# Second graph layer in half blocks of 128 edges: 416 steps of the edge loop instead of 428, two additions per step, lag of two

## The chip, the cores and the metric

The kernel runs on one core of one Trainium2 chip. The metric is the device time of one execution in microseconds; lower is better. Engines are named as in the profile: PE (TensorE), DVE (VectorE), ACT (ScalarE), POOL (GpSimd), SP (SyncE, which only issues DMAs here).

## What is computed

A small network over 3125 nodes and 103125 directed edges sorted by target node: a three-layer mean-aggregation graph network, a mixture of 16 experts, a relational graph layer, and a mixture of 8 experts, each behind a layer norm and added to the stream. The change concerns the third of the four. Cut to what matters:

```
m     = clifford_linear(h[src] * r[edge_type], msg_w, msg_b)   # per edge
m     = m * sigmoid(r[edge_type] @ gate_w + gate_b) * norm(src, dst)
h_agg = segment_sum(m, dst)                                     # per node
h_out = clifford_linear(h + h_agg, upd_w, upd_b)
x     = x + h_out
```

The linear map commutes with the sum over edges, so the kernel first sums `h[src] * r[type]` (with the gate and the norm of the source multiplied into the rows) over the edges of each node, 257 numbers per edge (256 features and the factor itself for the bias), and applies the weights once per node afterwards.

## The kernel before

Nodes stand in 25 tiles of 128 (`NT`). The sorted edges, padded to 808 x 128, are cut into `BLOCKS` = 404 blocks of `BLOCK` = 256 edges. A block belongs to the tile of its first edge; edges of it that lie in a later tile fall outside its one-hot matrix. For each of the `EDGES_AT` = 24 borders between tiles an extra block is run a second time for the later tile: `total` = 404 + 24 = 428 steps.

`edge_blocks` (L361 to L472), early in the program beside other work, turns the sorted list into tables: `b_src` (row to gather, per partition), `b_near` (place of the target in its tile), `b_tile` (tile of a block), `b_start` (first edge of an extra block). They are saved to HBM and loaded before the first use in `build`.

`aggregate` (L547 to L663) is the edge loop. One step n does:

- SP (L594): one DMA brings 256 rows of `relation_rows` (1040 bytes each, written by earlier stages) to `rel`; partition p gets rows 2p and 2p+1, 2080 bytes in a row.
- POOL (L608): two indirect DMAs gather 128 rows of `h_table` each into `rows`, with indices from `b_src`. POOL may be `SLOTS` = 12 steps ahead of PE (L605).
- ACT (L575, L578): two activations give |place - column|, one gives the two one-hot matrices, up to six steps ahead.
- DVE (L629): `rows` times `rel`, in place, both in SBUF. Ahead of it DVE's sequencer reads the tile number of step n-3 from `b_tile` into a register (L637, `value_load`).
- PE (L657): two fp32 matmuls, summed in one PSUM bank of six; the profile shows each as two MATMUL records.
- DVE (L623): adds the bank of step n-3 (`LAG` = 3) to the accumulator of its tile, in SBUF.

The waits are on counters: `s_sum` counts steps that PE has finished (plus 13 to begin with), `s_acc` additions, `s_ready` products. `Beside` puts a little other work (weights, and the part of the update that needs no sum, one node tile every 14 steps) into the same loop on PE, ACT and DVE. All loops are unrolled in the program; each engine runs its own list in order.

Of the kernel before, what the change touches and what calls it, by code (L numbers as in the profile page):

```python
# [57 lines left out]
SLOTS, BANKS, LAG = 12, 6, 3  # L58
assert PARTS * PER_PART == BLOCKS
# [301 lines left out]
def edge_blocks(nc, c, loads, relation):  # L361
# [5 lines left out]
    block_bits = BLOCK.bit_length() - 1  # L367
    with Core(nc) as k:
        both = k.sb("eb_lists", [PARTS, 2, PER_PART, BLOCK])
        first_i = k.sb("eb_first_i", [PARTS, 2, PER_PART], I32)  # L370
        base = k.sb("eb_base", [PARTS, PER_PART])
# [4 lines left out]
        pick = k.sb("eb_pick", [PARTS, PER_PART, EDGES_AT])  # L376
        n4 = k.sb("eb_n4", [PARTS, 1])
        near = k.sb("eb_near_in", [PARTS, 1, PER_PART, BLOCK])
        shift = k.sb("eb_shift", [P, EDGES_AT])
        src_out = k.sb("eb_src", [P, BLOCKS + EDGES_AT, 2], I32)  # L380
        near_out = k.sb("eb_near", [P, BLOCKS + EDGES_AT, 2])
# [6 lines left out]
        with nc.Block() as block:  # L388
# [11 lines left out]
            def _(sp):  # L400
                sp.dma_start(start[:, :], c.tab["a_start_d"]).then_inc(s_start, 16)
                sp.dma_start(both[:, :, :, :], c.lists.rearrange("a (n b e) -> n a b e", n=PARTS, b=PER_PART)).then_inc(s_lists, 16)
# [7 lines left out]
                sp.dma_start(c.tab["b_src_d"], src_out[:, :, :].rearrange("p g k -> p (g k)")).then_inc(s_saved, 16)  # L410
                sp.dma_start(c.tab["b_near_d"], near_out[:, :, :].rearrange("p g k -> p (g k)")).then_inc(s_saved, 16)
# [4 lines left out]
            def _(dve):  # L416
# [4 lines left out]
                v.tensor_scalar(at[:, 0, :], starts, block_bits, block_bits, ALU.arith_shift_right, ALU.logical_shift_left)  # L421
                v.tensor_scalar(at[:, 1, :], starts, block_bits, None, ALU.arith_shift_right)
                st.link(v.tensor_scalar(at[:, 2, :], starts, BLOCK - 1, None, ALU.bitwise_and))
# [10 lines left out]
                v.tensor_tensor(near[:, 0, :, :], bc(base[:, :].unsqueeze(2), [PARTS, PER_PART, BLOCK]), both[:, 1, :, :], ALU.subtract).then_inc(s_near, 1)  # L434
                dve.wait_ge(s_spread, 1)
                st.link(v.tensor_scalar_mul(n4[:, :], spread[0:PARTS, 64:65], float(PER_PART)))
                st.link(v.tensor_scalar(own[:, :], spread[0:PARTS, 0:EDGES_AT], n4[:, 0:1], None, ALU.subtract))
                for b in range(PER_PART):
                    last = v.tensor_scalar(pick[:, b, :], own[:, :], float(b), None, ALU.is_equal)
# [4 lines left out]
                for q in range(4):  # L444
                    out = src_out if q < 2 else near_out
                    view = out[:, 0:BLOCKS, q % 2].rearrange("p (n b) -> p b n", b=PER_PART)
                    v.tensor_copy(view, turned[:, q, 0:BLOCKS].rearrange("p (b n) -> p b n", b=PER_PART))
                dve.wait_ge(s_turn, 2)
                for q in range(2):
                    v.tensor_copy(src_out[:, BLOCKS:, q], extra[:, q * 32:q * 32 + EDGES_AT])  # L450
                    last = v.tensor_tensor(near_out[:, BLOCKS:, q], shift[:, :], extra[:, 64 + q * 32:64 + q * 32 + EDGES_AT], ALU.subtract)
                last.then_inc(s_out, 1)

            @block.tensor
            def _(pe):
# [6 lines left out]
                for q in range(4):  # L462
                    for b in range(PER_PART):
                        src = both[:, 0, b, q % 2:BLOCK:2] if q < 2 else near[:, 0, b, q % 2:BLOCK:2]
# [3 lines left out]
                for q in range(4):  # L468
                    for b in range(PER_PART):
                        last = nc.tensor.matmul(extra[:, q * 32:q * 32 + EDGES_AT], both[:, q // 2, b, q % 2:BLOCK:2], pick[:, b, :],  # L470
                                                start=b == 0, stop=b == PER_PART - 1)
# [75 lines left out]
def aggregate(nc, c, name, table, width, acc, relation_rows, kernels, beside):  # L547
# [4 lines left out]
    total = BLOCKS + EDGES_AT  # L552
    with Core(nc) as k:
        rows = k.sb(f"{name}_rows", [P, SLOTS, 2, width])
        rel = k.sb(f"{name}_rel", [P, SLOTS, 2, width])
        gap = k.sb(f"{name}_gap", [P, BANKS, 2, P])
        onehot = k.sb(f"{name}_onehot", [P, BANKS, 2, P])
# [5 lines left out]
        with nc.Block() as block:  # L563

            @block.scalar
            def _(act):
# [3 lines left out]
                def places(n):  # L570
                    g = n

                    act.wait_ge(s_sum, g + (SLOTS + 2 - BANKS))
                    for t in range(2):
                        last = nc.scalar.activation(gap[:, n % BANKS, t, :], c.iota[:, 0:P], ACT.Abs, bias=c.tab["b_near"][:, bass.ds(g * 2 + t, 1)])  # L575
                    last.then_inc(s_gap, 1)
                    act.wait_ge(s_gap, g + 1)
                    nc.scalar.activation(onehot[:, n % BANKS, :, :], gap[:, n % BANKS, :, :], ACT.Relu, bias=1.0, scale=-1.0).then_inc(s_oh, 1)  # L578
# [10 lines left out]
            def _(sp):  # L589
                def relation(n, start):  # L590

                    sp.wait_ge(s_sum, (n + 2))
                    src = relation_rows[bass.ds(start, BLOCK), :].rearrange("(p k) c -> p (k c)", p=P)
                    sp.dma_start(rel[:, n % SLOTS, :, :].rearrange("p k c -> p (k c)"), src).then_inc(s_rel[n % SLOTS], 16)  # L594
# [20 lines left out]
            def _(dve):  # L615
                v = nc.vector

                def add(g, bank, tile):

                    dve.wait_ge(s_acc, g + BANKS)  # L620
                    dve.wait_ge(s_sum, g + (SLOTS + 2 - LAG))
                    here = acc[:, bass.ds(tile, 1), 0:used].rearrange("p a d -> p (a d)")
                    v.tensor_tensor(here, here, sums[:, bank, 0:used], ALU.add).then_inc(s_acc, 1)  # L623

                def block_of(g, n, uses, tile):
                    dve.wait_ge(s_rel[n % SLOTS], uses * 16)
                    dve.wait_ge(s_rows[n % SLOTS], uses * 32)
                    here = rows[:, n % SLOTS, :, 0:used]
                    v.tensor_tensor(here, here, rel[:, n % SLOTS, :, 0:used], ALU.mult).then_inc(s_ready, 1)  # L629
                    add(g, (n - LAG) % BANKS, tile)  # L630

                v.memset(c.tab["b_tile"][:, 0:LAG], NT).then_inc(s_acc, 1)
                v.memset(acc[:, :, :], 0.0).then_inc(s_acc, BANKS - 1)
                dve.wait_ge(s_acc, BANKS)
                for n in range(total):
                    if n - LAG < BLOCKS:
                        tile = dve.value_load(c.tab["b_tile"][0:1, n:n + 1], min_val=0, max_val=NT)  # L637
                    else:
                        tile = n - LAG - BLOCKS + 1
                    block_of(n, n, n // SLOTS + 1, tile)  # L640
                    beside.vector(dve, v, n)
                for n in range(total, total + LAG):
                    add(n, (n - LAG) % BANKS, n - LAG - BLOCKS + 1)

            @block.tensor
            def _(pe):

                for q in range(LAG):
# [1657 lines left out]
def build(nc, I, out):  # L2306
    with Core(nc) as c:
# [19 lines left out]
        block_tables = {"b_src": ([P, (BLOCKS + EDGES_AT) * 2], I32), "b_near": ([P, (BLOCKS + EDGES_AT) * 2], F32),  # L2327
# [110 lines left out]
```

## Time and profile before

| | us |
|---|---|
| median of 3 runs | 3507.81 (3500.52 to 3517.4) |
| the profiled execution | 3519.02, of it span 3517.0 |
| edge loop of the second graph layer, first gather to last addition | 1798.6 to 2929.4 |
| POOL busy over the span | 2005.0 (57%) |
| PE busy over the span | 2505.9 (71%) |
| DVE, ACT busy over the span | 1375.3 (39%), 1405.1 (40%) |

The edge loop is about a third of the span. Shares over the whole span say little about it; the rows further down are taken from inside it. Columns of a group of instructions: line, engine, operation, output<-input, count, then busy time in total and mean of one, then the idle time of the engine just before such instructions and what ended most of it.

### The profile page before, as it was taken

To read this page: it belongs to the slowest core of one execution; us is meant where nothing else is said; L and a number is where in the kernel's file an instruction comes from. 1 tells how busy PE (TensorE), PEld (TensorE's weight loads), DVE (VectorE), ACT (ScalarE), POOL (GpSimd) and SP (SyncE) were. 2 spreads that over 40 slices of the span, in tenths; PEclk is the share of its full clock that TensorE was granted. 3 is DMA by queue.
4 is the path that set the end of the run, shared out by engine and by line. 5 is a ranking of instruction groups with operands and counts; after the bars stand their busy time and mean duration, and the time that the engine had idled before them with its cause. 6 is when DMAs were issued, how large, how long until landed. Compare 5 with 4: busy or idle time off the path is not lost. (4 is left out here: it accounts for less than half of the span.)

```text
span 3517.0 us, 51132 instructions
## 1 busy us (share of the span) xinstructions
PE 2505.9 (71%) x14080; PEld 1923.5 (55%) x14080; DVE 1375.3 (39%) x4123; ACT 1405.1 (40%) x3615; POOL 2005.0 (57%) x1969
## 2 busy tenths in 40 slices
PE   0156899999999847886016666666667667499997
PEld 0123566678888746875014444444444445488986
DVE  4167789942221150000864444444444445500100
ACT  0035666646740022322034444444444443255554
POOL 0454767667777136653647777777777771033332
PEclk9998999999999958998557766776766667599998
DMA  2674676678888336665347777777777771354233
GB/s 111 202 253 122 199 211 197 209 220 263 265 259 243 105 118 190 186 200 156 96 152 211 202 206 198 200 206 204 200 203 203 203 207 59 117 174 129 37 82 62
DMA packets 343366, 620.94 MB, mean 177 GB/s; under 512 B 82286, under 2 KB 157565, under 8 KB 342241
## 3 DMA queue, kind: packets, MB, share of 16 engines
q1 hardware_dynamic: 236033, 343.11, 30.2%
q0 software_dynamic: 101360, 268.76, 28.9%
q10 hardware_dynamic: 5728, 6.11, 0.5%
q8 instruction: 115, 1.88, 0.2%
q14 instruction: 130, 1.06, 0.1%
HBM read 451.74 MB, written 170.90 MB: 177 GB/s over the span
## 5 line engine op out<-in xcount | busy, mean ns | idle before, releaser
L608 POOL DMA_INDIRECT agg_r_rows<-h_table,parts_and_x x856 | 864.9, 1010 | 315.3 <-issue 217.6
L657 PE MATMUL agg_r_sums<-agg_r_rows,agg_r_onehot 128*128 128x257 f32 x1712 | 702.3, 560 | 388.9 <-DVE agg_r_rows L629 329.1
L657 PEld LDWEIGHTS agg_r_sums<-agg_r_rows,agg_r_onehot 128*128 128x128 f32 x1712 | 432.3, 276 | 645.6 <-issue 580.4
L1414 POOL DMA_INDIRECT rl_buf<-r_table,kinds x608 | 626.6, 1031 | 261.9 <-issue 171.4
L629 DVE TENSOR_TENSOR agg_r_rows<-agg_r_rows,agg_r_rel 128x514 f32<-128x514 f32 x428 | 298.9, 698 | 649.8 <-DMA agg_r_rows<-h_table,parts_and_x 648.0
L575 ACT ACTIVATE agg_r_gap<-iota,parts_and_x 128x128 f32<-128x128 f32 x856 | 295.2, 392 | 520.8 <-PE agg_r_sums L657 489.8
L1784 PE MATMUL f_pH<-f_xT,f_w 128*128 128x128 f32 x2816 | 369.4, 292 | 79.5 <-DMA f_w<-in_L_ffn_w 55.5
L1784 PEld LDWEIGHTS f_pH<-f_xT,f_w 128*128 128x128 f32 x2816 | 353.6, 205 | 110.9 <-DMA f_w<-in_L_ffn_w 60.3
L1136 PE MATMUL ly_acc<-parts,matrix 128*128 128x256 bf16 x1250 | 342.2, 274 | 0.0
L1135 PE MATMUL ly_acc<-parts,matrix 128*128 128x256 bf16 x1250 | 340.4, 272 | 0.0
L1134 PE MATMUL ly_acc<-parts,matrix 128*128 128x257 bf16 (+1 forms) x1250 | 340.2, 272 | 0.0
L1869 ACT ACTIVATE f_hT<-f_pH,f_b 128x128 f32<-128x128 f32 x704 | 197.8, 372 | 345.6 <-PE f_pH L1784 345.3
L1803 PE MATMUL f_pY<-f_w,f_hT 128*128 128x256 f32 x1408 | 327.1, 382 | 0.0
L1803 PEld LDWEIGHTS f_pY<-f_w,f_hT 128*128 128x128 f32 x1408 | 262.1, 193 | 30.9
L2022 POOL DMA_INDIRECT f_xb<-xn_table,f_token x120 | 118.2, 985 | 246.0 <-DVE f_home L1970 116.3
L2010 POOL DMA_INDIRECT f_ys<-f_yb,f_home x56 | 88.2, 1575 | 294.6 <-DVE f_yb L1995 263.7
L1272 DVE TENSOR_SCALAR b_oh<-b_numbers,b_code 128x400 bf16<-128x400 f16 x980 | 254.6, 324 | 0.0
L1123 PE MATMUL b_strips<-b_oh,b_at 128*128 128x400 bf16 x980 | 200.8, 336 | 63.4 <-DVE b_oh L1272 30.3
L1414 POOL DMA_INDIRECT f_rr_buf<-r_table,kinds x120 | 121.4, 1012 | 150.7 <-POOLq L113 112.8
L623 DVE TENSOR_TENSOR acc<-acc,agg_r_sums 128x257 f32 (+1 forms) x431 | 179.2, 416 | 13.2 <-PE agg_r_sums L657 13.1
L578 ACT ACTIVATE agg_r_onehot<-agg_r_gap 128x256 f32<-128x256 f32 x428 | 178.3, 416 | 13.5
L1989 DVE TENSOR_TENSOR f_plain<-f_pY,f_b 128x256 f32<-128x256 f32 x56 | 23.8, 424 | 380.5 <-PE f_pY L1803 380.5
(389 smaller groups left out, 3543.2 us busy)
## 6 DMA issues: line engine op xcount, KB each, us to landing
agg_r_rel<-relation_rows SPq DMA_DIRECT2D x428, 260.0 KB, 3.1
relation_rows<-rl_buf SPq DMA_DIRECT2D x304, 260.0 KB
f_w<-in_L_ffn_W SPq DMA_DIRECT2D x28, 1024.0 KB, 5.8
f_w<-in_L_ffn_w SPq DMA_DIRECT2D x38, 512.0 KB, 5.9
relation_rows<-f_rr_buf POOLq DMA_DIRECT2D x60, 260.0 KB, 2.6
agg_r_rows<-h_table,parts_and_x POOLq DMA_INDIRECT x856, 3.4
ly_zin<-zh SPq DMA_DIRECT2D x50, 256.0 KB
zh<-ly_out SPq DMA_DIRECT2D x50, 256.0 KB, 2.7
```

The costliest lines, as they stand in the source:

```text
L575: last = nc.scalar.activation(gap[:, n % BANKS, t, :], c.iota[:, 0:P], ACT.Abs, bias=c.tab["b_near"][:, bass.ds(g * 2 + t, 1)])
L608: pool.indirect_dma_start(rows[:, n % SLOTS, t, :], None, table, bass.IndirectOffsetOnAxis(ap=indices[:, t:t + 1], axis=0)).then_inc(s_row ...
L629: v.tensor_tensor(here, here, rel[:, n % SLOTS, :, 0:used], ALU.mult).then_inc(s_ready, 1)
L657: last = nc.tensor.matmul(sums[:, n % BANKS, 0:used], onehot[:, n % BANKS, t, :], rows[:, n % SLOTS, t, 0:used], start=t == 0, stop=t == 1)
L1123: last = nc.tensor.matmul(strips[:, n % BANKS, 0:CODES], at[:, n % 2, t, :], oh[:, n % 2, t, :], start=t == 0, stop=t == DEEP - 1)
L1134: nc.tensor.matmul(acc[:, n % 2, 0:D + one], m[:, s, own], of[:, s, 2 * D:3 * D + one], start=s == 0, stop=False)
L1135: nc.tensor.matmul(acc[:, n % 2, 0:D], m[:, s, own], of[:, s, 0:D], start=False, stop=False)
L1136: last = nc.tensor.matmul(acc[:, n % 2, 0:D], m[:, s, own], of[:, s, D:2 * D], start=False, stop=s == NT - 1)
L1272: last = v.tensor_scalar(oh[:, n % 2, t, :], numbers[:, :], code[:, q, 1, own, t:t + 1], None, ALU.is_equal)
L1414: pool.indirect_dma_start(self.buf[:, n, g, :], None, self.table, bass.IndirectOffsetOnAxis(ap=self.c.kinds[:, at:at + 1], axis=0)).then_i ...
L1784: last = nc.tensor.matmul(pH[s][:, f * P:(f + 1) * P], w1b[:, s, h, f * P:(f + 1) * P], xT[:, s, h, :], start=h == 0, stop=h == KD - 1)
L1803: last = nc.tensor.matmul(pY[s][:, 0:D], hT[:, s, f, :], w2b[:, s, f, :], start=f == 0, stop=f == FC - 1)
```

## The change

Halves of 128 edges take the place of the block as the unit that belongs to a tile: `HALVES` = 808. A step still handles 256 edges, now two halves, each with a tile of its own, so each half has a PSUM bank and an addition of its own. The 24 borders need 24 extra halves, which make 12 steps; `total` = 404 + 12 = 416. `LAG` goes from 3 to 2, so six banks hold three steps of two banks. `HOT` = 6 keeps the ring of one-hot matrices as it was. The relation rows of a half go one to a partition: 1040 bytes to `rel[p, 0]` and 1040 to `rel[p, 1]`, from places 128 rows apart; an extra step fetches its two halves with two DMAs from two start addresses. DVE reads two tile numbers per step, and it does so behind the product of the step. `edge_blocks` builds the tables in the new order.

```diff
-SLOTS, BANKS, LAG = 12, 6, 3
+SLOTS, BANKS, LAG, HOT = 12, 6, 2, 6
+HALVES, PER_HALF = 2 * BLOCKS, 2 * PER_PART
...
-    total = BLOCKS + EDGES_AT
+    total = BLOCKS + EDGES_AT // 2
...
                 for n in range(BLOCKS):
-                    relation(n, n * BLOCK)
+                    sp.wait_ge(s_sum, n + 2)
+                    src = relation_rows[n * BLOCK:(n + 1) * BLOCK, :].rearrange("(k p) c -> p k c", p=P)
+                    sp.dma_start(rel[:, n % SLOTS, :, :], src).then_inc(s_rel[n % SLOTS], 16)
                 for n in range(BLOCKS, total):
-                    relation(n, sp.value_load(c.tab["b_start"][0:1, n - BLOCKS:n - BLOCKS + 1], min_val=0, max_val=EDGE_TILES * P))
+                    starts = [sp.value_load(c.tab["b_start"][0:1, at:at + 1], min_val=0, max_val=EDGE_TILES * P)
+                              for at in (2 * (n - BLOCKS), 2 * (n - BLOCKS) + 1)]
+                    sp.wait_ge(s_sum, n + 2)
+                    for t in range(2):
+                        sp.dma_start(rel[:, n % SLOTS, t, :], relation_rows[bass.ds(starts[t], P), :]).then_inc(s_rel[n % SLOTS], 16)
...
+                def tile_of(half):
+                    at = half + 2 * LAG
+                    return dve.value_load(c.tab["b_tile"][0:1, at:at + 1], min_val=0, max_val=NT) if half < HALVES else half - HALVES + 1
+                def add(n):
+                    tiles = [tile_of(2 * (n - LAG) + t) for t in range(2)]
+                    dve.wait_ge(s_sum, n + (SLOTS + 2 - LAG))
+                    for t in range(2):
+                        dve.wait_ge(s_acc, 2 * n + t + BANKS)
+                        here = acc[:, bass.ds(tiles[t], 1), 0:used].rearrange("p a d -> p (a d)")
+                        v.tensor_tensor(here, here, sums[:, (2 * (n - LAG) + t) % BANKS, 0:used], ALU.add).then_inc(s_acc, 1)
...
-                for q in range(LAG):
+                for q in range(2 * LAG):
                     last = nc.tensor.matmul(sums[:, BANKS - 1 - q, 0:used], c.zero_b[:, 0:P], c.zero_b[:, 0:used], start=True, stop=True)
...
-                    pe.wait_ge(s_acc, g + (LAG + 1))
+                    pe.wait_ge(s_acc, 2 * (g + LAG + 1))
...
-                        last = nc.tensor.matmul(sums[:, n % BANKS, 0:used], onehot[:, n % BANKS, t, :], rows[:, n % SLOTS, t, 0:used],
-                                                start=t == 0, stop=t == 1)
+                        last = nc.tensor.matmul(sums[:, (2 * n + t) % BANKS, 0:used], onehot[:, n % HOT, t, :], rows[:, n % SLOTS, t, 0:used],
+                                                start=True, stop=True)
```

On DVE, in the middle of the edge loop, one step before the change reads as follows: the register load of a tile number, the product, the register operations that carry the waits of the addition, the addition. `acc1` is the accumulator, `b_tile` the table of tile numbers.

```order
L637 TENSOR_LOAD b_tile
L637 ISA x2
L629 TENSOR_TENSOR agg_r_rows<-agg_r_rows,agg_r_rel 128x2x257
L623 ISA
L623 TENSOR_TENSOR acc1<-acc1,agg_r_sums 128x257
```

The same engine and place with the change (L642 is the product, L623 the tile number, L633 the addition):

```order
L642 TENSOR_TENSOR agg_r_rows<-agg_r_rows,agg_r_rel 128x2x257
L623 TENSOR_LOAD b_tile
L623 ISA x2
L623 TENSOR_LOAD b_tile
L623 ISA x2
L633 ISA
L633 TENSOR_TENSOR acc1<-acc1,agg_r_sums 128x257
L633 ISA
L633 TENSOR_TENSOR acc1<-acc1,agg_r_sums 128x257
```

Two loads with their register operations now stand between the product and the first addition; before, the one load stood between an addition and the next product.

On SP, the relation rows: first the 404 regular steps, then one extra step, before the change.

```order
L594 DMA agg_r_rel<-relation_rows 128x520 x404
L599 TENSOR_LOAD parts_and_x
L599 ISA x2
L594 ISA
L594 DMA agg_r_rel<-relation_rows 128x520
```

With the change:

```order
L592 DMA agg_r_rel<-relation_rows 128x2x260 x404
L594 TENSOR_LOAD parts_and_x
L594 ISA x2
L594 TENSOR_LOAD parts_and_x
L594 ISA x2
L598 ISA
L598 DMA agg_r_rel<-relation_rows 128x260
L598 ISA
L598 DMA agg_r_rel<-relation_rows 128x260
```

Each regular DMA carries the same bytes in twice as many pieces; an extra step loads two start addresses and issues two DMAs of half the size.

## Rows read from the trace of the kernel before

**Rows 1.** Page, part 5: groups of the edge loop on POOL, PE, DVE, ACT.
```profile
L608 POOL DMA_INDIRECT agg_r_rows<-h_table,parts_and_x x856 | 864.9, 1010 | 315.3 <-issue 217.6
L657 PE MATMUL agg_r_sums<-agg_r_rows,agg_r_onehot 128*128 128x257 f32 x1712 | 702.3, 560 | 388.9 <-DVE agg_r_rows L629 329.1
L629 DVE TENSOR_TENSOR agg_r_rows<-agg_r_rows,agg_r_rel 128x514 f32<-128x514 f32 x428 | 298.9, 698 | 649.8 <-DMA agg_r_rows<-h_table,parts_and_x 648.0
L575 ACT ACTIVATE agg_r_gap<-iota,parts_and_x 128x128 f32<-128x128 f32 x856 | 295.2, 392 | 520.8 <-PE agg_r_sums L657 489.8
L623 DVE TENSOR_TENSOR acc<-acc,agg_r_sums 128x257 f32 (+1 forms) x431 | 179.2, 416 | 13.2 <-PE agg_r_sums L657 13.1
L578 ACT ACTIVATE agg_r_onehot<-agg_r_gap 128x256 f32<-128x256 f32 x428 | 178.3, 416 | 13.5
```

**Rows 2.** Line 608, its gathers: duration in ns min/median/max, first and last start.
```profile
L608 POOL DMA_INDIRECT agg_r_rows<-h_table,parts_and_x x856: 949/953/1472, 1798.6 to 2923.1; - x172
```

**Rows 3.** Timeline of the loop's end: start, duration, engine, [idle before <-what ended it].
```profile
2916.56 0.42 DVE L623 TENSOR_TENSOR acc<-acc,agg_r_sums 128x257 f32<-128x257 f32 x1
...
2916.83 0.95 POOL L608 DMA_INDIRECT agg_r_rows<-h_table,parts_and_x  x1 [0.31 <-issue]
...
2926.57 1.33 DVE L623 TENSOR_TENSOR acc<-acc,agg_r_sums 128x257 f32<-128x257 f32 x3
...
2926.81 2.05 PE L657 MATMUL agg_r_sums<-agg_r_rows,agg_r_onehot 128*128 128x257 f32 x4 [0.43 <-DVE agg_r_rows L629]
2928.97 0.42 DVE L623 TENSOR_TENSOR acc<-acc,agg_r_sums 128x257 f32<-128x257 f32 x1 [1.06 <-PE agg_r_sums L657]
```

**Rows 4.** Timelines of POOL and DVE where a gather is long and where not.
```profile
2033.44 1.29 POOL L608 DMA_INDIRECT agg_r_rows<-h_table,parts_and_x  x1 [0.30 <-issue]
...
2033.22 0.69 DVE L629 TENSOR_TENSOR agg_r_rows<-agg_r_rows,agg_r_rel 128x514 f32<-128x514 f32 x1 [1.83 <-DMA agg_r_rows<-h_table,parts_and_x]
...
2603.13 0.95 POOL L608 DMA_INDIRECT agg_r_rows<-h_table,parts_and_x  x1 [0.30 <-PE agg_r_sums L657]
2603.25 0.69 DVE L629 TENSOR_TENSOR agg_r_rows<-agg_r_rows,agg_r_rel 128x514 f32<-128x514 f32 x1 [1.37 <-DMA agg_r_rows<-h_table,parts_and_x]
```

**Rows 5.** Line 637, the register load on DVE's sequencer: ns min/median/max.
```profile
L637 DVEq TENSOR_LOAD <-b_tile x407: 298/304/330, 1804.0 to 2869.5; - x136
L637 DVEq FUSED_REGOPS  x407: 190/190/190, 1804.4 to 2869.9; - x136
L637 DVEq SEQ_ASSERT  x407: 23/23/33, 1804.6 to 2870.1; - x136
```

**Rows 6.** Timeline of DVE: two steps back to back, and additions in a chain.
```profile
2515.35 0.70 DVE L629 TENSOR_TENSOR agg_r_rows<-agg_r_rows,agg_r_rel 128x514 f32<-128x514 f32 x1 [2.98 <-DMA agg_r_rows<-h_table,parts_and_x]
2515.96 0.42 DVE L623 TENSOR_TENSOR acc<-acc,agg_r_sums 128x257 f32 x1
2516.30 0.69 DVE L629 TENSOR_TENSOR agg_r_rows<-agg_r_rows,agg_r_rel 128x514 f32<-128x514 f32 x1
...
2509.61 0.41 DVE L2287 TENSOR_TENSOR parts_and_x<-parts_and_x,be_result 128x256 f32<-128x256 f32 x1
2510.06 0.42 DVE L2289 TENSOR_TENSOR parts_and_x<-parts_and_x,upd_bias 128x256 f32<-128x256 f32 x1
```

**Rows 7.** DMA queues and issues from 2000 to 2800 us: packets, MB, share of 16 engines.
```profile
q0 software_dynamic: 29118, 80.81, 38.0%
q1 hardware_dynamic: 43742, 80.89, 34.0%
...
agg_r_rel<-relation_rows SPq DMA_DIRECT2D x304, 260.0 KB, 3.0
agg_r_rows<-h_table,parts_and_x POOLq DMA_INDIRECT x609, 3.4
```

**Rows 8.** DMA queue from 1790 to 1797 us, a store of 1040-byte rows.
```profile
q1 hardware_dynamic: 656, 0.67, 27.3%
```

**Rows 9.** Timeline: that store's issue, and the matmuls ahead of the first gather.
```profile
1792.18 0.36 SPq L2129 DMA_DIRECT2D h_table<-f_out  x1
...
1796.92 0.81 PE L649 MATMUL agg_r_sums<-zero_b 128*128 128x257 bf16 x3 [133.55 <-PEq L113]
```

**Rows 10.** Timeline of the end of `edge_blocks`.
```profile
165.71 0.17 DVE L451 TENSOR_TENSOR eb_near<-eb_shift,eb_extra 128x24 f32<-128x24 f32 x1
...
169.84 7.90 SPq L410 DMA_DIRECT2D b_src_d<-eb_src  x1
```

More of the change, by code:

```diff
@@ L57 @@
 PARTS, PER_PART = 101, 4
-SLOTS, BANKS, LAG = 12, 6, 3
-assert PARTS * PER_PART == BLOCKS
+SLOTS, BANKS, LAG, HOT = 12, 6, 2, 6
+HALVES, PER_HALF = 2 * BLOCKS, 2 * PER_PART
+assert PARTS * PER_PART == BLOCKS and EDGES_AT % 2 == 0 and BANKS % 2 == 0 and LAG < BANKS // 2
 E0, F0, TILES0 = 16, 512, (2 * N + 16 * (P - 1)) // P
@@ L433, in _ @@
                 st.link(v.tensor_scalar_mul(base[:, :], base[:, :], float(P)))
-                v.tensor_tensor(near[:, 0, :, :], bc(base[:, :].unsqueeze(2), [PARTS, PER_PART, BLOCK]), both[:, 1, :, :], ALU.subtract).then_inc(s_near, 1)
+                v.tensor_tensor(near[:, :, :], bc(base[:, :].unsqueeze(2), [PARTS, PER_HALF, P]), both[:, 1, :, :], ALU.subtract).then_inc(s_near, 1)
                 dve.wait_ge(s_spread, 1)
-                st.link(v.tensor_scalar_mul(n4[:, :], spread[0:PARTS, 64:65], float(PER_PART)))
+                st.link(v.tensor_scalar_mul(n4[:, :], spread[0:PARTS, 64:65], float(PER_HALF)))
                 st.link(v.tensor_scalar(own[:, :], spread[0:PARTS, 0:EDGES_AT], n4[:, 0:1], None, ALU.subtract))
-                for b in range(PER_PART):
+                for b in range(PER_HALF):
                     last = v.tensor_scalar(pick[:, b, :], own[:, :], float(b), None, ALU.is_equal)
@@ L445, in _ @@
                     out = src_out if q < 2 else near_out
-                    view = out[:, 0:BLOCKS, q % 2].rearrange("p (n b) -> p b n", b=PER_PART)
+                    view = out[:, 0:HALVES].rearrange("p (n b) -> p b n", b=PER_HALF)[:, (q % 2) * PER_PART:(q % 2 + 1) * PER_PART, :]
                     v.tensor_copy(view, turned[:, q, 0:BLOCKS].rearrange("p (b n) -> p b n", b=PER_PART))
                 dve.wait_ge(s_turn, 2)
[L449 to L452, printed above, removed]
+                v.tensor_copy(src_out[:, HALVES:], extra[:, 0:EDGES_AT])
+                v.tensor_tensor(near_out[:, HALVES:], shift[:, :], extra[:, 32:32 + EDGES_AT], ALU.subtract).then_inc(s_out, 1)
             @block.tensor
@@ L463, in _ @@
                     for b in range(PER_PART):
-                        src = both[:, 0, b, q % 2:BLOCK:2] if q < 2 else near[:, 0, b, q % 2:BLOCK:2]
+                        half = (q % 2) * PER_PART + b
+                        src = both[:, 0, half, :] if q < 2 else near[:, half, :]
                         last = nc.tensor.transpose(turned[:, q, b * PARTS:(b + 1) * PARTS], src, c.ident[0:PARTS, 0:PARTS])
@@ L467, in _ @@
                 pe.wait_ge(s_pick, 1)
[L468 to L471, printed above, removed]
+                for q in range(2):
+                    for b in range(PER_HALF):
+                        last = nc.tensor.matmul(extra[:, q * 32:q * 32 + EDGES_AT], both[:, q, b, :], pick[:, b, :],
+                                                start=b == 0, stop=b == PER_HALF - 1)
                 last.then_inc(s_turn, 1)
@@ L616, in _, with loads_of @@
                 v = nc.vector
[L618 to L632, printed above, removed]
+                def loads_of(n):
+                    slot = [q for q in range(n + 1) if q % SLOTS == n % SLOTS]
+                    return sum(16 if q < BLOCKS else 32 for q in slot)
+                def tile_of(half):
[8 more added lines that the diff above has]
+                        v.tensor_tensor(here, here, sums[:, (2 * (n - LAG) + t) % BANKS, 0:used], ALU.add).then_inc(s_acc, 1)
+                v.memset(c.tab["b_tile"][:, 0:2 * LAG], NT).then_inc(s_acc, 1)
                 v.memset(acc[:, :, :], 0.0).then_inc(s_acc, BANKS - 1)
@@ L635, in _ @@
                 for n in range(total):
[L636 to L640, printed above, removed]
+                    dve.wait_ge(s_rel[n % SLOTS], loads_of(n))
+                    dve.wait_ge(s_rows[n % SLOTS], (n // SLOTS + 1) * 32)
+                    here = rows[:, n % SLOTS, :, 0:used]
+                    v.tensor_tensor(here, here, rel[:, n % SLOTS, :, 0:used], ALU.mult).then_inc(s_ready, 1)
+                    add(n)
                     beside.vector(dve, v, n)
                 for n in range(total, total + LAG):
-                    add(n, (n - LAG) % BANKS, n - LAG - BLOCKS + 1)
+                    add(n)
             @block.tensor
             def _(pe):
-                for q in range(LAG):
+                for q in range(2 * LAG):
                     last = nc.tensor.matmul(sums[:, BANKS - 1 - q, 0:used], c.zero_b[:, 0:P], c.zero_b[:, 0:used], start=True, stop=True)
```

49 lines of the change are left out of this document (22 added, 27 removed).

## The prediction

> **What bounds the kernel now.** The change touches one stage, the edge loop, so I read that stage first by its groups [rows 1]. Per step of 256 edges (428 of them) the engines are busy: POOL 864.9 / 428 = 2.02 us, PE 702.3 / 428 = 1.64 us, DVE (298.9 + 179.2) / 428 = 1.12 us, ACT (295.2 + 178.3) / 428 = 1.11 us. None fills a step of about 2.6 us by busy time alone, so the idle columns decide. DVE's idle time ahead of the product is ended by the gathered rows landing (648.0 of 649.8 us), PE's mostly by DVE's product, ACT's by PE: all three wait down one chain that begins at POOL. POOL's own idle time is ended by "issue", and in the timelines each gap before a gather is 0.30 or 0.31 us, also where the page names PE as the releaser [rows 3, 4]: PE's count had been reached, and the 0.30 us is what POOL's own queue needs between two gathers. So POOL issues without a real wait from 1798.6 to 2923.1 us [rows 2], and its pace is the stage's: (2923.1 - 1798.6) / 855 = 1.315 us a gather, 2.63 us a step.
>
> A gather takes 0.95 us at the median but 1.010 in the mean, up to 1.47 [rows 1, 2]. The long ones sit where DVE's product had begun shortly before the gather (product at 2033.22, gather at 2033.44: 1.29 us); a product that begins after the gather does nothing to it (gather 2603.13, product 2603.25: 0.95 us) [rows 4]. An addition still running when a gather starts does not lengthen it either (2916.56 + 0.42 reaches past 2916.83; 0.95 us) [rows 3]. All this costs 856 x (1.010 - 0.953) = 49 us in the loop.
>
> **The change, part by part.**
>
> 1. *Twelve steps fewer.* 24 gathers go from the queue that sets the pace: 24 x 1.315 = 31.6 us less. The share of held gathers is inside the 1.315, and goes with the products, which also become 12 fewer. Everything else of those steps lay beside POOL.
>
> 2. *A second addition per step on DVE.* One reads PSUM and SBUF like the first, which did not hold a gather [rows 3]. The Trainium skill says the same and says why (SBUF — State Buffer, "Who interferes with whom"): a DVE instruction with at most one SBUF input doesn't contend with GpSimd, one with two SBUF inputs does contend with a GpSimd instruction that reads SBUF. It adds that a tensor_tensor had not been seen to stall a GpSimd-issued DMA; rows 4 show that it does here, and the measurement decides. By either the second addition costs POOL nothing.
>
> 3. *DVE's minimal step.* Today two products can follow each other by 0.95 us [rows 6], far below 2.63. Now the two tile numbers are read behind the product. One read is 0.304 + 0.190 + 0.023 us on DVE's sequencer, with gaps some 0.62 (the assert starts 0.6 us after the load: 1804.0 to 1804.6) [rows 5]. Does it run while the product does? 2515.35 to 2516.30 holds a product, an addition and a whole read, which fits into 0.95 us only if the read lies beside the product and the addition [rows 6]. So from the product's start: two reads to 1.3, register operations of the address and dispatch some 0.15 (estimate from the rest of the 0.95 us) to 1.5, the first addition; the second waits for it, as L2289 waits for L2287, 0.45 later [rows 6], 0.1 more for its own address: 2.05; the next product 0.34 us after an addition's start (2515.96 to 2516.30) [rows 6]: 2.4 us. Bounds: 1.53 = 0.70 + 2 x 0.416 if the reads cost nothing, 3.0 if they start only when the product has ended (0.70 + 1.24 + 0.13 + 0.55 + 0.34). I take 2.4, since rows 6 show the overlap. The update of a node tile adds 2 x 0.42 us every 14 steps, 0.05 a step: 2.45 against POOL's 2.63. DVE becomes 93% full but not the pace. Products will start later after landing now and then; POOL is allowed 12 steps ahead of PE and is now only some three ahead (landing 3.4 us, product 0.70, matmuls 2.05), so nine steps, over 20 us, hide that.
>
> 4. *Lag of two.* The additions of step n need the matmuls of n-2. Two minimal steps are 4.8 us; product and matmuls are 0.70 + 2.05 us [rows 3]: done 2 us before. PE waits for two more additions than before, but they stand on DVE ahead of the product that PE waits for anyway. Cost nil; the cover, should DVE get slower, grows with it. PE's work per step is the same two matmuls, only into two banks. Where its duration changed with the bank it would have 2.63 - 2.05 us of room.
>
> 5. *Relation rows in pieces of 1040 bytes.* 304 loads took 34.0% of 16 engines for 800 us: 0.34 x 16 x 800 / 304 = 14.3 us of engine time, 0.90 us of all 16 per step; per 2080-byte piece (128 a load) 112 ns under this load. The gathers: 38.0%, 1.00 us a step. Sum 1.90 of 2.63 us [rows 7]. Alone, a 1040-byte packet took 0.273 x 16 x 7 / 656 = 47 ns [rows 8]. Bounds for the new load: 256 x 47 / 16 = 0.75 us and 256 x 112 / 16 = 1.79 us (each small piece as long as a large one). The nearest row is the gathers, the same 1040-byte rows at the same bytes per step in the same stage: 1.00 us. I take that: DMA 2.0 of 2.63 us, not the bound. The load is issued nine steps ahead, so a longer landing costs nothing. SP needs 0.36 us to issue a DMA of 640 such rows [rows 9]; it has room.
>
> 6. *Extra steps on SP.* Two register loads and two DMAs per step, 12 times: under 2 us of SP in 2.63, and steps ahead. Nil.
>
> 7. *The ends.* One zero matmul more ahead of the first gather: 0.81 / 3 = 0.3 us [rows 9]. The last step ends with two additions: +0.5 us (part 3) on 2928.97 [rows 3].
>
> 8. *`edge_blocks`.* Four small comparisons more, a copy and an addition fewer; the tables are ready at 165.9 us, and SP stores them only from 169.8 [rows 10]: 4 us of cover. Nil; without it, well under 1 us.
>
> **Sum.** -31.6 + 0.3 + 0.5 = -30.8 us. The profiled execution of 3519.02 would take 3488.2. It lay 11.2 us above the median of the runs; from the median 3507.81 I get 3477.0 us, -0.88%. What a measurement can tell from no change is 0.5%, 17.5 us: faster is below 3490.3, slower above 3525.3.
>
> **Rivals.**
>
> A. *DVE becomes the pace, slower than before.* If the reads of tile numbers do not run beside the product, the step is 3.0 us plus 0.05: 416 x 3.05 = 1269 against the 1125 of now, +144 us, 3652. For it speaks only that no row shows a read directly behind a product with an empty queue; against it the 0.95 us of rows 6. It decides from 2.70 us a step (416 x 2.70 = 1123), and is slower by over 0.5% from 2.745. Chance 0.04. A page has a figure of its own here: the Trainium skill (DMA: Bandwidth & Descriptors, "Latency and other measured facts") gives a tensor_load a floor of about 600 ns. By it the estimate would be 2.4 + 0.6 = 3.0 us and the change slower; rows 5 measure 304 ns for the same instruction, so the measurement decides and that adds no chance.
>
> B. *The same, but only just.* A step of 2.6 to 2.745 us by a gap or two that I haven't seen (I have 0.18 us of room): at 2.70, some 3507. Chance 0.10.
>
> C. *DMA becomes the pace.* Pieces at 112 ns: 1.79 + 1.00 = 2.79 us a step, 416 x 2.79 = 1161, +36 us, 3544. Against it [rows 7, 8]. Chance 0.02. The Trainium skill (same page, "Why small descriptors are slow") lays the price on a fixed overhead of some three cycles per packet, next to nothing at 1040 bytes, which goes with the lower bound.
>
> D. *The beat of products and gathers shifts.* Held gathers cost 49 us. They depend on when a product starts relative to the next gather. With DVE nearly full, products no longer start only on a landing. Should they miss the gathers, up to 48 us more are gained (3430); should twice as many be hit, 49 are lost and the gain turns into +18 (3526). Landing times spread over more than one beat of 1.315 us, so I expect the share to stay. Chance 0.02 each way.
>
> **How the numbers follow.** The forecast has 0.80, its own range 3466 to 3490 (runs of one kernel spread by 17 us, a shift of the held gathers by a fifth is 10). Faster: 0.80 + 0.02 = 0.82. Same: B, 0.10. Slower: A, C and half of D, 0.08. The range of 8 in 10 reaches into B: 3463 to 3504.
>
> **What would show it.** L608 x832 with a mean near 1.01 us and gaps of 0.30; the stage some 31 us shorter. DVE: additions x836 at 0.42; a minimal distance of products near 2.4 us; its idle before the product falls from 649.8 to under 250 us and is still ended by the gathers. If instead POOL shows gaps longer than 0.31 us with PE as releaser, A, B or C holds: C if the DMA share is near 1, A or B if DVE has no idle time. A mean gather away from 1.01 is D. Queue q1 near 256 data packets a load, its share near 38%. I would be wrong above 3490.

## Result and the profile after

| | before | changed |
|---|---|---|
| median of runs, us | 3515.45 (7 runs, 3500.52 to 3517.4) | 3481.69 (7 runs, 3475.51 to 3491.04) |
| profiled execution, us | 3519.02, span 3517.0 | 3475.51, span 3473.7 |
| edge loop, us | 1798.6 to 2929.4: 1130.8 | 1789.5 to 2889.4: 1099.9 |

The ratio is 0.9916, with a 95% interval from 0.9899 to 0.9933: 0.84% faster. Forecast were 3477.0 us, 0.88% less, and a range from 3463 to 3504. The loop became 30.9 us shorter in the profiled executions, against 30.8 in the sum. That the two agree to 0.1 us is luck, since single executions differ by more (see "The twelve steps alone"). The profiled executions as a whole differ by 43.5 us. The other 12.6 lie outside the loop: 9.1 ahead of it, the rest behind it. Ahead of it the change touches only `edge_blocks`, whose tables are ready at 165.2 us (165.9 before). The loops of the eight other profiled kernels on chips of this speed begin anywhere from 1790.5 to 1797.9 us, so the 9.1 us are put down to spread between executions; that isn't shown.

The groups of the loop in the profile after (columns as in [rows 1]):

```profile
L607 POOL DMA_INDIRECT agg_r_rows<-h_table,parts_and_x x832 | 841.1, 1011 | 308.2 <-issue 220.1
...
L633 DVE TENSOR_TENSOR acc<-acc,agg_r_sums 128x257 f32 (+1 forms) x836 | 353.5, 423 | 351.5 <-issue 239.5
...
L642 DVE TENSOR_TENSOR agg_r_rows<-agg_r_rows,agg_r_rel 128x514 f32<-128x514 f32 x416 | 289.5, 696 | 97.7 <-DMA agg_r_rows<-h_table,parts_and_x 95.0
```

POOL does 24 gathers fewer at the old price (1.011 against 1.010 us, gaps of 0.30 to 0.31). DVE's idle time ahead of the product fell from 649.8 [rows 1] to 97.7 us. In exchange 351.5 us of waiting appeared ahead of the additions, most of it "issue": the reads of tile numbers. Line 607 shows the pace, (2883.0 - 1789.5) / 831 = 1.316 us a gather, 1.315 before [rows 2]:

```profile
L607 POOL DMA_INDIRECT agg_r_rows<-h_table,parts_and_x x832: 949/953/1470, 1789.5 to 2883.0; - x167
```

The timeline of DVE where work is queued, and the last step:

```profile
2182.08 0.69 DVE L642 TENSOR_TENSOR agg_r_rows<-agg_r_rows,agg_r_rel 128x514 f32<-128x514 f32 x1
2183.54 1.00 DVE L633 TENSOR_TENSOR acc<-acc,agg_r_sums 128x257 f32 x2 [0.76 <-issue]
2184.45 0.69 DVE L642 TENSOR_TENSOR agg_r_rows<-agg_r_rows,agg_r_rel 128x514 f32<-128x514 f32 x1
2185.68 1.00 DVE L633 TENSOR_TENSOR acc<-acc,agg_r_sums 128x257 f32 x2 [0.54 <-issue]
2186.59 0.69 DVE L642 TENSOR_TENSOR agg_r_rows<-agg_r_rows,agg_r_rel 128x514 f32<-128x514 f32 x1
...
2888.56 0.88 DVE L633 TENSOR_TENSOR acc<-acc,agg_r_sums 128x257 f32<-128x257 f32 x2 [0.20 <-PE agg_r_sums L660]
```

Two products follow each other by 2.37 and by 2.14 us; the first addition starts 1.23 to 1.46 us after the product. The two reads of the step that begins at 2184.45 start at 2184.2 and 2184.9 on DVE's sequencer. So they do run beside the product (and the first already beside the addition ahead of it), but now reach past it.

The DMA queues from 2000 to 2800 us, against [rows 7]:

```profile
q0 software_dynamic: 29182, 80.98, 37.6%
q1 hardware_dynamic: 82433, 80.71, 35.4%
```

Twice the data packets for the same 304 loads raised the share of q1 from 34.0% to 35.4%, which is 0.93 us of 16 engines a step.

### The profile page after: what moved, and what is told of

Read it like the earlier page. It is cut to its first block and busy times, and to the rows that moved or that the text cites. A ratio compares the mean times of both kernels' runs of the same rounds, so it can differ in the third digit from the quotient of the medians.

```text
span 3473.7 us, 52944 instructions
## 1 busy us (share of the span) xinstructions
PE 2487.7 (72%) x14033; PEld 1898.7 (55%) x14033; DVE 1557.4 (45%) x4518; ACT 1391.9 (40%) x3579; POOL 1988.8 (57%) x1945
## 5 line engine op out<-in xcount | busy, mean ns | idle before, releaser
L607 POOL DMA_INDIRECT agg_r_rows<-h_table,parts_and_x x832 | 841.1, 1011 | 308.2 <-issue 220.1
L660 PE MATMUL agg_r_sums<-agg_r_rows,agg_r_onehot 128*128 128x257 f32 x1664 | 684.5, 555 | 371.8 <-DVE agg_r_rows L642 317.4
L660 PEld LDWEIGHTS agg_r_sums<-agg_r_rows,agg_r_onehot 128*128 128x128 f32 x1664 | 410.9, 271 | 630.9 <-issue 351.2
L633 DVE TENSOR_TENSOR acc<-acc,agg_r_sums 128x257 f32 (+1 forms) x836 | 353.5, 423 | 351.5 <-issue 239.5
L574 ACT ACTIVATE agg_r_gap<-iota,parts_and_x 128x128 f32<-128x128 f32 x832 | 287.0, 392 | 480.6 <-PE agg_r_sums L660 449.3
L1787 PE MATMUL f_pH<-f_xT,f_w 128*128 128x128 f32 x2816 | 359.4, 287 | 77.8 <-DMA f_w<-in_L_ffn_w 54.5
L1787 PEld LDWEIGHTS f_pH<-f_xT,f_w 128*128 128x128 f32 x2816 | 343.2, 200 | 109.7 <-DMA f_w<-in_L_ffn_w 60.2
L642 DVE TENSOR_TENSOR agg_r_rows<-agg_r_rows,agg_r_rel 128x514 f32<-128x514 f32 x416 | 289.5, 696 | 97.7 <-DMA agg_r_rows<-h_table,parts_and_x 95.0
```

Source lines behind the costliest of these rows:

```text
L574: last = nc.scalar.activation(gap[:, n % HOT, t, :], c.iota[:, 0:P], ACT.Abs, bias=c.tab["b_near"][:, bass.ds(g * 2 + t, 1)])
L607: pool.indirect_dma_start(rows[:, n % SLOTS, t, :], None, table, bass.IndirectOffsetOnAxis(ap=indices[:, t:t + 1], axis=0)).then_inc(s_row ...
L633: v.tensor_tensor(here, here, sums[:, (2 * (n - LAG) + t) % BANKS, 0:used], ALU.add).then_inc(s_acc, 1)
L660: last = nc.tensor.matmul(sums[:, (2 * n + t) % BANKS, 0:used], onehot[:, n % HOT, t, :], rows[:, n % SLOTS, t, 0:used], start=True, stop= ...
L1787: last = nc.tensor.matmul(pH[s][:, f * P:(f + 1) * P], w1b[:, s, h, f * P:(f + 1) * P], xT[:, s, h, :], start=h == 0, stop=h == KD - 1)
```

## Experiments

Each ratio is to runs of the kernel before on the same chip at the same time. "Held" below is the number of gathers times (mean - 0.953 us). In the profiles of three kernels (twelve steps alone, both reads ahead of the product, first gate) the undisturbed gather, the median, takes 0.957 us, so there it comes out some 3 us too high.

**The twelve steps alone.** The kernel before, 416 steps, the last 12 border blocks left out.

```diff
-    total = BLOCKS + EDGES_AT
+    total = BLOCKS + EDGES_AT // 2
```

> The kernel before with the last 12 of its 24 extra blocks left out (416 steps instead of 428; the sums of twelve tiles then lack their border edges), nothing else changed. My theory, POOL's gathers set the pace: 24 gathers fewer at 1.315 us, so 31.6 us less than before, the whole of the change's gain (ratio near 0.991), with the gap before a gather still 0.30 us. Rival, the new code itself (banks, lag, register loads) brings or costs something: then this kernel differs from the changed one by more than 0.3%.

Measured: 3485.13 us, ratio 0.9925 [0.9908, 0.9942]; the changed kernel has 0.9916 [0.9899, 0.9933]. The two intervals overlap almost wholly: the gain is the twelve steps, and the rest of the new code is worth nothing that can be measured. Its profile shows a mean gather of 1.022, so 57 us held, 9 more than the changed kernel. Single executions of loops that hardly differ held 48 to 57 us (48 in the changed kernel, 52 in its first gated form, 57 here and in the next kernel), so a few us of difference in this share say nothing.

```profile
L608 POOL DMA_INDIRECT agg_r_rows<-h_table,parts_and_x x832 | 850.3, 1022 | 307.8 <-issue 206.0
```

**Relation rows in large pieces.** The changed kernel, its 404 regular loads in 2080-byte pieces.

```diff
-src = relation_rows[n * BLOCK:(n + 1) * BLOCK, :].rearrange("(k p) c -> p k c", p=P)
-sp.dma_start(rel[:, n % SLOTS, :, :], src).then_inc(s_rel[n % SLOTS], 16)
+src = relation_rows[n * BLOCK:(n + 1) * BLOCK, :].rearrange("(p k) c -> p (k c)", p=P)
+sp.dma_start(rel[:, n % SLOTS, :, :].rearrange("p k c -> p (k c)"), src).then_inc(s_rel[n % SLOTS], 16)
```

> The changed kernel with the relation rows of the 404 regular steps loaded as before, in pieces of 2080 bytes, two neighbouring rows to a partition (the product then pairs rows with other edges' relations). POOL theory: DMA is not the bound, so no change of time against the changed kernel (ratio to before still near 0.991), only the share of queue q1 in the middle of the loop falls from 35.4% to some 34%. Rival, small pieces cost: the loop gets shorter by up to the difference in DMA time.

Measured: 3488.15 us, ratio 0.9941 [0.9923, 0.9960], not faster than the changed kernel (0.9916); its profiled execution had a mean gather of 1.021. The share of q1 in the same window is 33.6%. Small pieces cost DMA time and no time of the kernel that these runs can tell.

```profile
q1 hardware_dynamic: 43350, 80.17, 33.6%
```

**Both reads ahead of the product.**

```diff
+def tiles_of(n):
+    return [tile_of(2 * (n - LAG) + t) for t in range(2)]
...
 for n in range(total):
+    tiles = tiles_of(n)
     dve.wait_ge(s_rel[n % SLOTS], loads_of(n))
...
-    add(n)
+    add(n, tiles)
```

> The changed kernel with both tile numbers read ahead of the waits of the product, as the kernel before did with its one. POOL theory: DVE gets idle time back (its wait between product and addition, 0.75 us, goes; the minimal distance of two products falls from 2.11 to some 1.5 us), the time stays within 0.3% of the changed kernel. Rival, DVE is at times the pace after the change: some us are gained.

Measured: 3461.64 us, ratio 0.9858 [0.9841, 0.9876], 20 us faster than the changed kernel. My theory fell on both counts: DVE's step did not get shorter, and the time changed. The rival's outcome came (some us gained), but not for its reason, as DVE's step got longer. The timelines of POOL and then DVE, the same microseconds:

```profile
2304.25 0.95 POOL L607 DMA_INDIRECT agg_r_rows<-h_table,parts_and_x  x1 [0.30 <-PE agg_r_sums L663]
...
2306.77 0.96 POOL L607 DMA_INDIRECT agg_r_rows<-h_table,parts_and_x  x1 [0.31 <-issue]
...
2304.35 0.70 DVE L645 TENSOR_TENSOR agg_r_rows<-agg_r_rows,agg_r_rel 128x514 f32<-128x514 f32 x1 [0.92 <-issue]
2304.96 0.99 DVE L635 TENSOR_TENSOR acc<-acc,agg_r_sums 128x257 f32 x2
2306.86 0.69 DVE L645 TENSOR_TENSOR agg_r_rows<-agg_r_rows,agg_r_rel 128x514 f32<-128x514 f32 x1 [0.92 <-issue]
```

The register operation with the second addition's address waits for the first addition (it runs at 2305.4), and the reads stand behind it: they start at 2305.5 and 2306.2 on DVE's sequencer, and the last check at 2306.7. The second addition (2305.5 to 2305.9) is all that runs beside them, since the product now stands behind them. That leaves 0.92 us of idle time ahead of the product and a step of 2.51 us. Two gathers that nobody holds take as long (2306.77 - 2304.25 = 2.52). Where the rows are taken, the two loops run in step and the product starts 0.1 us into a gather. Over the whole loop held gathers almost vanish:

```profile
L607 POOL DMA_INDIRECT agg_r_rows<-h_table,parts_and_x x832 | 804.0, 966 | 321.1 <-issue 225.0
```

(1.011 - 0.966) x 832 = 37 us less held. Some of it is given back, since DVE is now a pace of its own: with the 0.83 us of a node tile in 14 steps its step is 2.57 us, and (2863.6 - 1794.4) / 416 is 2.57. POOL's gaps add 321.1 - 308.2 = 13 us, and from the last gather to the last addition it takes 17.6 us instead of 6.4. That leaves 13 us for the loop (1086.7 against 1099.9). The profiled executions differ by 10.6 us and the medians by 20; where the rest of the 20 lies is not shown.

**Four reads instead of two**, the extra two unused.

```diff
 tiles = [tile_of(2 * (n - LAG) + t) for t in range(2)]
+for t in range(2):
+    tile_of(2 * (n - LAG) + t)
```

> The changed kernel with two more register loads per regular step behind the product, results unused: 1.24 us more on DVE's sequencer, its minimal step from 2.11 (measured; 2.34 is common) to 3.35 to 3.6 us. Theory, the loads cost nothing as long as DVE's step stays under POOL's 2.63 and everything above it: 404 steps x (3.35 to 3.6 - 2.63) = +290 to +390 us against the changed kernel. Rival, the loads overlap with DVE's work and cost little: below +100 us.

This kernel (like the next one, and two gated ones further down) ran on a chip on which the kernel before took 4088.87 us; ratios there don't compare with the others. Measured: ratio 1.0469 [1.0405, 1.0532], 4284.44 us, 148 us above the next kernel on the same chip. The changed kernel did not run there, so the time can't be read against +290 to +390 us; the mechanism can. Groups from 2400 to 3400 us:

```profile
L607 POOL DMA_INDIRECT agg_r_rows<-h_table,parts_and_x x578 | 601.0, 1040 | 400.7 <-PE agg_r_sums L662 290.7 <-issue 110.0
...
L644 DVE TENSOR_TENSOR agg_r_rows<-agg_r_rows,agg_r_rel 128x514 f32<-128x514 f32 x289 | 199.5, 690 | 0.1
```

The product never waits (0.1 us in 1000), POOL waits for PE: DVE is the pace, at 1000 / 289 = 3.46 us a step, inside the expected 3.35 to 3.6. The whole loop took 1452.7 us, 353 more than the changed kernel's on the first chip, which would fit the expectation, but compares two chips. Rival A's mechanism, DVE as the pace, exists; two reads just don't reach it.

**A lag of one.**

```diff
-SLOTS, BANKS, LAG, HOT = 12, 6, 2, 6
+SLOTS, BANKS, LAG, HOT = 12, 6, 1, 6
```

> The changed kernel with a lag of one step instead of two. The additions of step n then need the matmuls of n-1, which start after the product of n-1; two reads stand between product and additions. Theory: a lag of two has room and a lag of one is just about enough at the pace of 2.63 us: matmuls of n-1 end 0.70 + 2.05 = 2.75 us after product n-1, additions of step n could start at 2.63 + 1.4 = 4.0, so under 0.3% change against the changed kernel, and DVE's waits on PE rise from 35 us to some 100. Rival, the lag is part of what sets the time: over 1% slower.

On that other chip: 4136.33 us, ratio 1.0119 [1.0062, 1.0177]. The changed kernel itself was not run there, so the price of the lag stays open. DVE's waits for PE ahead of the additions were 76.8 us in 1000 (in the changed kernel, on the first chip, 34.9 us in 980).

**Gating the product on POOL's count.** Three forms on the changed kernel, two on the kernel before. `s_gate` is POOL's own count of steps, which both kernels raise ahead of a step's two gathers (L605 in the changed kernel, L606 in the kernel before). None of the forms gated anything, as the rows behind the last ones show.

```diff
 dve.wait_ge(s_rows[n % SLOTS], (n // SLOTS + 1) * 32)
+dve.wait_ge(s_gate, min(n + 4, total))
```

> The changed kernel in which the product of step n also waits for POOL's own count of steps, raised while the first gathers of step n+3 are in sight, some 0.3 us after a gather has begun; the product then starts inside a gather and not just ahead of one. Theory, a product that starts in the 0.57 us ahead of a gather holds the gather until 0.57 us into the product: held gathers cost 48.5 us now; with the products moved most of it goes, mean gather from 1.011 to under 0.98 us, 25 to 48 us less (3435 to 3457 against 3482). Rival, the length of gathers has another cause (DMA rings, load on HBM) and only coincides with products: mean gather stays 1.01 and the time is the same or a little longer.

Measured: 3478.99 us, ratio 0.9910 [0.9895, 0.9925], mean gather 1.016. No gain. Next with a read between wait and product:

```diff
 dve.wait_ge(s_gate, min(n + 4, total))
+first = tile_of(2 * (n - LAG))
...
-tiles = [tile_of(2 * (n - LAG) + t) for t in range(2)]
+tiles = [first, tile_of(2 * (n - LAG) + 1)]
```

> The changed kernel with the product of step n held back until POOL's count for step n+3, and with the first of the two tile numbers read between that wait and the product. The count is raised 0.28 us ahead of a gather (2305.230 against 2305.511 in the first gated kernel, whose products therefore still began just ahead of gathers), a read takes 0.62 us: the product should start some 0.4 us into a gather. Theory, products that start in the 0.57 us ahead of a gather hold it: held gathers fall from 48.5 us to under 10, mean gather to 0.96, no backlog as DVE's step of some 2.2 us is below POOL's 2.51; stage near 1055 us, time near 3440. Rival, the order or the number of reads on DVE made the kernel with the reads first quicker (3461.6): then this one, with one read first, lies between that and the changed kernel (3461 to 3482) with gathers as long as before.

> The kernel before (428 steps, one addition) with the waits of the product and POOL's count put ahead of its register load, so that its product too starts some 0.4 us into a gather. Theory: its held gathers (49 us) go, its gain is about that, 3511 to some 3465, and the changed kernel with the same wait stays 24 x 1.257 = 30 us ahead of it. Rival, the held gathers belong to the changed loop's rhythm alone: no gain here.

Both on the other chip: 4146.93 us, ratio 1.0157 [1.0112, 1.0202], and for the kernel before with the gate 4093.20 us, 1.000 [0.9968, 1.0033]. The first was run again on a chip on which the kernel before takes 3509.4 us:

> The same kernel as the second gated one (product held back until POOL's count for step n+3, one of the two reads between wait and product); its first runs fell on a chip on which the kernel before took 4089 us, and POOL waited for landed rows there. On a chip where the kernel before takes some 3510 us: theory of the held gathers as before, mean gather 0.96, gap 0.30, time near 3440; rival, between 3461 and 3482 with gathers of 1.01 us.

Measured: 3463.92 us, ratio 0.9865 [0.9827, 0.9904], mean gather 0.997, a quarter of the holding gone. Then a later count, in both kernels (the second edit is that of the kernel before):

```diff
-dve.wait_ge(s_gate, min(n + 4, total))
+dve.wait_ge(s_gate, min(n + 5, total))
```

```diff
...
 for n in range(total):
+    dve.wait_ge(s_rel[n % SLOTS], (n // SLOTS + 1) * 16)
+    dve.wait_ge(s_rows[n % SLOTS], (n // SLOTS + 1) * 32)
+    dve.wait_ge(s_gate, min(n + 5, total))
     if n - LAG < BLOCKS:
         tile = dve.value_load(c.tab["b_tile"][0:1, n:n + 1], min_val=0, max_val=NT)
...
-    dve.wait_ge(s_rel[n % SLOTS], uses * 16)
-    dve.wait_ge(s_rows[n % SLOTS], uses * 32)
```

> The gated changed kernel with one read ahead of the product, now waiting for POOL's count of step n+4 instead of n+3. In the run with n+3 many products still began on a late landing and not on the count (held gathers 36.9 us, time 3463.9). Step n+4 is counted 4 x 2.51 - 0.28 = 9.8 us after the first gather of step n, past nearly all landings. Theory: held gathers 5 to 15 us (left over after each node tile's 0.83 us of extra DVE work), stage near 1062 us, 3440 to 3452. Rival: the later wait fills the ring of 12 steps and POOL waits for PE, gaps above 0.31 us, no gain over 3464.

> The kernel before (428 steps) with the waits of its product, and POOL's count of step n+4, put ahead of its one register load. Theory: DVE's minimal step stays far below POOL's, so products sit some 0.4 us into a gather at nearly every step; held gathers 49 us to under 5, mean gather 0.955, stage 856 x 1.258 + 6 = 1083 us, time 3511 to some 3463. That would show that holding is not the changed loop's alone, and leave 24 x 1.258 = 30 us of gain for the twelve steps. Rival: no gain.

Measured: 3459.20 us, ratio 0.9853 [0.9832, 0.9874], mean again 0.997, so a later count changed nothing; and 3523.72 us, ratio 1.0038 [1.0023, 1.0053], mean 1.022, for the kernel before with the gate. The reason is in the trace. L606 is POOL's count in the latter kernel, L608 the gathers:

```profile
L606 POOLq EVENT_SEMAPHORE  x428: 17/17/17, 1795.2 to 2914.1; - x143
L608 POOL DMA_INDIRECT agg_r_rows<-h_table,parts_and_x x856: 949/953/1476, 1796.0 to 2930.8; - x172
```

The last step is counted at 2914.1 us, and its two gathers start 15 to 17 us later. POOL's sequencer passes the count when it hands the gathers on, and in the middle of the loop that is 6 to 7 steps, some 16 us, before they start. That a count falls 0.28 us ahead of a gather is true, but the gather is one of an earlier step. Put step by step against the products, the awaited count had stood for at least 4 us at every product of all the gated runs, and for 11 us or more at the median. So the gate never ended a wait, and these kernels test something else: the first is the changed kernel again (0.9910 against 0.9916), and the others move a read between the waits and the product.

Read so, one read ahead of the product instead of two behind it is worth something: 3463.92 and 3459.20 us, 18 and 22 below the changed kernel. In the profiled executions the gathers take 11.6 us less in all, and the loops are 11.7 us shorter (1088.2 and 1088.3 us). In the kernel before, the read held up the product a little and did not help: mean gather 1.022 against 1.010 is 856 x 0.012 = 10 us, its loop is 9.9 us longer, and it is 13.7 us slower than the kernel before beside it (3510.0). In each the loop's time goes with the mean gather. Why one order holds fewer gathers than the other is not shown, and no run placed the product inside the gathers on purpose.

**The product left out.** A copy of one number per partition stands in its place; the sums are of the bare rows.

```diff
-v.tensor_tensor(here, here, rel[:, n % SLOTS, :, 0:used], ALU.mult).then_inc(s_ready, 1)
+v.tensor_copy(rows[:, n % SLOTS, 0, 0:1], rel[:, n % SLOTS, 0, 0:1]).then_inc(s_ready, 1)
```

> The changed kernel with the product left out (a copy of one number per partition stands in its place and raises the count, so the sums are of the bare rows). Theory: no DVE instruction with two SBUF inputs is left in the loop but one in 14 steps, so gathers are no longer held (mean 0.953 to 0.96 instead of 1.011) and POOL's pace is 1.257 us a gather; 832 x 0.058 = 48 us less than the changed kernel, 3434. Rival, the long gathers come from DMA: mean stays 1.01, time as the changed kernel's.

Measured: 3431.16 us, ratio 0.9773 [0.9733, 0.9814].

```profile
L607 POOL DMA_INDIRECT agg_r_rows<-h_table,parts_and_x x832 | 793.1, 953 | 308.2 <-issue 225.5 <-PE agg_r_sums L651 54.9 <-PE agg_r_sums L659 27.7
```

The mean gather is the undisturbed 0.953, the gaps are as before (308.2), and the time is 50 us below the changed kernel against 48 expected; the loop is 1051.2 us against 1099.9. DMA moved the same bytes, so DMA does not lengthen gathers. It is the product, and POOL is the pace: shorten its instruction, and the kernel gets shorter by as much. Only three of the 832 gathers are still over 1 us. Each follows an addition of the node tile's update, one in 14 steps, which has both operands in SBUF, like the product (the longest one, timelines of DVE and POOL):

```profile
2787.56 0.42 DVE L2291 TENSOR_TENSOR parts_and_x<-parts_and_x,upd_bias 128x256 f32<-128x256 f32 x1
2787.65 1.17 POOL L607 DMA_INDIRECT agg_r_rows<-h_table,parts_and_x  x1 [0.30 <-issue]
```

The profiled execution of the changed kernel says the same, gather by gather. In 148 gathers the last product had started 0.05 to 0.55 us earlier. All of these are long (0.97 to 1.47 us), and lead and duration add up to 1.51 to 1.53 us in each. They make up 46.7 of the 48.3 us held. Of the 648 gathers with a lead over 0.6 us seven are over 0.97 us, and each of the seven follows that addition of the update.

## Why the prediction was right

- *Part 1, twelve steps.* Right in mechanism and size: 24 gathers at 1.315 us. The kernel before with 416 steps brings the same by itself (26 us by the medians, 34 for the change, with intervals that overlap). The price was read off a loop that held 49 us, and the changed one held 48.
- *Part 2, the second addition costs POOL nothing.* Right: mean gather 1.011 with twice the additions, and 0.953 with all of them and no product.
- *Part 3, DVE's step.* Taken as 2.4 us, bounds 1.53 and 3.0; measured 2.14 to 2.37 where work is queued. The term that was too large is the stretch from the product to the first addition, 1.5 us in the sum and 1.23 to 1.46 measured, because the first read can start ahead of the product. My account of the overlap was right for this order only. I would have sized the order with both reads first at 1.5 us; it takes 2.51, because what a read is queued behind counts as much as how long it takes.
- *Part 4, lag of two.* No cost shown; PE ended 34.9 us of DVE's waits ahead of the additions (in 980 us), and POOL's gaps stayed. How near a lag of one is, is open.
- *Part 5, pieces of 1040 bytes.* Taken as 1.00 us a step, bounds 0.75 and 1.79; measured 0.93, not the bound. The sign named for it, a share of q1 near 38%, missed: 35.4%.
- *Part 7, the ends.* The second of the last two additions costs 0.88 - 0.42 = 0.46 us, forecast 0.5.
- *Part 8, `edge_blocks`.* Its tables are ready at 165.2 us and SP stores `b_src` from 168.7, so there is cover as forecast.
- *Rivals.* A needs more than two reads (four get there). B and C did not occur. D, with 0.02 to each side, was the one I mispriced: the beat is worth up to 48 us, and an innocent change of order moved it by 37. It stayed at 48.5 us here, as forecast, but I had no reason beyond the spread of landings. That part of the hit is luck: with both reads ahead of the product, which the prediction's account would not have told apart, the same change would have come out at 3461.64 us, below the range.

The quickest kernels that compute the whole result are those with fewer reads behind the product: 3459.20 and 3463.92 us (one read ahead of the product, with a gate that never held anything) and 3461.64 us (both ahead). They take 0.9853, 0.9865 and 0.9858 of the kernel before, 0.5 to 0.6% less than the changed kernel, and can't be told from each other.

## What to carry to other kernels

In a loop with one engine that never really waits (its gaps all equal the 0.30 us between two instructions of its queue), the price of a step is that engine's instructions times their pace, and an engine with room can take on work for nothing until its own shortest step reaches that pace. Work that shortest step out from the order of register reads, address operations and waits, not from busy time: DVE was busy 1.5 us a step and needed 2.14 to 2.51. When one engine can hold up the instruction of the one that sets the pace, look at where the two fall in each other's beat: here up to 48 us lay in it, 20 of which one move of two reads brought, against some 30 for the change. And before a counter is used to place one engine's work against another's, look in the trace when it is raised: here that was 16 us before the work that it was meant to mark.

## What the runs showed of the hardware

- A DVE product of two SBUF operands (0.70 us) that starts 0.05 to 0.57 us ahead of a GpSimd gather lengthens it, from 0.95 to as much as 1.47 us: it ends 1.52 us after the product's start, whatever the lead. With a lead under 0.05 us 20 of 23 gathers were not held, and a product that starts after the gather does nothing. Behind the shorter instruction of the update (0.42 us) the three long gathers of the kernel without a product end 1.25 us after its start. In both, the gather is as late as if it had begun some 0.13 us before the DVE instruction ended. Without the product the mean fell from 1.011 to 0.953 us.
- DVE additions with one operand in PSUM don't do it: in the kernel without the product 252 gathers began within 0.4 us of the start of such an addition, and none took over 0.97 us.
- A register read from SBUF takes DVE's sequencer 0.30 us, with its check 0.6, and runs beside an instruction in execution, but not past a register operation that waits for one (the step of 2.51 us).
- POOL's sequencer runs ahead of its gathers: it passed the semaphore operation ahead of a step's gathers some 16 us, 6 to 7 steps, before the first of them started.
- On another chip the kernel before took 4089 instead of 3511 us. The kernel before has no profile there, but its gated form, which takes as long (4093.20 us), has one: against the profile before, 454 us of the difference lie ahead of the edge loop, 129 in it (1260.0 against 1130.8 us), and POOL waits up to 5.0 us at a time. The two kernels of the changed family that differ least from it were 1.2% (lag of one) and 1.6% (one read ahead) slower than the kernel before there instead of faster, and their loops took 1312 and 1317 us. In the gated kernel before, products follow each other by 0.98 us where work is queued (2823.82, 2824.80), in the changed loop by 2.14 (2823.09, 2825.23, lag of one). That DVE's lost room is what costs there is argued, not shown.
